# Last expert stage: the second part's row scatter waits for the shared network's last output

## The reference

```python
shared = new_gelu(xf @ Wfc_s + bfc_s) @ Wproj_s + bproj_s
logits = xf @ Wr
probs = jax.nn.softmax(logits, axis=-1)
topk_p, topk_i = jax.lax.top_k(probs, TOP_K)
topk_p = topk_p / jnp.sum(topk_p, axis=-1, keepdims=True)
...
for e in range(N_EXPERTS):
    h = new_gelu(xf @ Wfc[e] + bfc[e]) @ Wproj[e] + bproj[e]
    routed = routed + h * gate[:, e:e + 1]
return (shared + routed).reshape(Bb, Tt, C)
```

## Time and profile before

| | us |
|---|---|
| median of three runs | 6130.41 (6125.94 to 6135.96) |
| span of the profiled execution, first to last instruction | 6118.5 |
| this phase in it, first to last instruction | about 5434.7 to 6118.5 |
| shared network's last output (L1970) | 5706.85 |
| last tile's bias (L2144) | 6044.6 |

### The profile page before, as it was taken

One profiled execution on the slowest core, in us unless ns is written; L12 is line 12 of the kernel. 1 busy time (PEld: TensorE's weight loads), 2 busy tenths in 40 slices (PEclk: granted clock), 3 DMA queues, 4 the chain that ended last, 5 costly groups with the idle time before them and its releaser, 6 DMA issues. The chain is left out here.

```text
span 6118.5 us, 105868 instructions
## 1 busy us (share of the span) xinstructions
PE 5082.0 (83%) x38217; PEld 2622.6 (43%) x38217; DVE 3494.7 (57%) x5632; ACT 3177.6 (52%) x7160; POOL 2473.6 (40%) x2086
## 2 busy tenths in 40 slices
PE   6999789898977999997999999874237999974995
PEld 2444234344424666643566664442112222241784
DVE  5787422577845666643666654565338999730233
ACT  2666633366764666642566663342014888841552
POOL 3333000222216888831888871016562232116025
PEclk7999999799987999998999999886567999976997
DMA  3443111233410000020000000011112333211123
GB/s 102 111 119 111 41 45 50 64 103 107 115 32 20 8 7 6 5 82 19 8 6 6 7 3 4 2 42 27 36 35 68 90 90 97 59 46 49 52 78 91
DMA packets 329515, 312.95 MB, mean 51 GB/s; under 512 B 78758, under 2 KB 279106, under 8 KB 327106
## 3 DMA queue, kind: packets, MB, share of 16 engines
q1 hardware_dynamic: 312642, 285.77, 16.4%
q0 software_dynamic: 16384, 20.69, 1.3%
HBM read 172.15 MB, written 136.32 MB: 50 GB/s over the span
## 5 line engine op out<-in xcount | busy, mean ns | idle before, releaser
L806 ACT ACTIVATE a_prob<-a_PB 128x512 f32<-128x512 f32 x2304 | 1253.1, 597 | 453.0 <-PE a_PB L648 337.5
L696 PE MATMUL a_PO<-a_prob,a_V 128*32 128x256 f32 (+3 forms) x8192 | 713.3, 421 | 22.6 <-ACT a_cn L779 22.3
L960 DVE TENSOR_REDUCE a_blocks<-a_PA 128x8 f32<-128x1024 f32 x512 | 602.1, 1215 | 37.6 <-PE a_PA L648 35.1
L963 DVE TENSOR_REDUCE a_neg<-a_PA 128x2 f32<-128x1024 f32 x512 | 591.0, 1213 | 34.5 <-PE a_PA L661 34.5
L661 PE MATMUL a_PA<-a_KS,a_QS 48*128 48x512 bf16 (+3 forms) x3072 | 470.4, 345 | 109.7 <-DVE a_blocks L960 68.5
L2534 DVE TENSOR_REDUCE f1a_neg<-f1a_PA 128x2 f32<-128x384 f32 (+1 forms) x512 | 267.1, 522 | 489.1 <-PE f1a_PA L2336 488.6
L2464 POOL TENSOR_TENSOR f1a_prob<-f1a_prob,f1a_inv 128x384 f32<-128x384 f32 (+1 forms) x512 | 395.3, 775 | 283.4 <-DVE f1a_inv L2538 283.4
L678 PE MATMUL a_PB<-a_QS,a_KS 51*128 51x512 bf16 (+3 forms) x3072 | 447.7, 329 | 57.2 <-ACT a_prob L806 55.3
L2428 ACT ACTIVATE f1a_pt<-f1a_PT 128x512 f32<-128x512 f32 (+1 forms) x512 | 278.8, 544 | 348.5 <-PE f1a_PT L2345 344.8
L2421 ACT ACTIVATE f1a_prob<-f1a_PA,f1a_neg 128x192 f32<-128x192 f32 (+1 forms) x1024 | 406.2, 405 | 68.0 <-DVE f1a_neg L2534 67.9
L661 PEld LDWEIGHTS a_PA<-a_KS,a_QS 48*128 48x128 bf16 x3072 | 123.6, 94 | 632.8 <-DVE a_blocks L960 200.3
(11 more groups left out here) (422 smaller groups left out, 10380.5 us busy)
## 6 DMA issues: line engine op xcount, KB each, us to landing
a_spill<-a_qkp SPq DMA_DIRECT2D x96, 384.0 KB
a_QS<-a_spill SPq DMA_DIRECT2D x384, 96.0 KB, 2.5
a_KS<-a_spill SPq DMA_DIRECT2D x384, 96.0 KB, 2.5
a_spill<-a_qkp SPq DMA_DIRECT2D x96, 256.0 KB
a_raw<-a_cn SPq DMA_DIRECT2D x192, 72.0 KB
a_spill<-a_qkp SPq DMA_DIRECT2D x96, 128.0 KB
f_rows<-tokens_in SPq DMA_DIRECT2D x78, 128.0 KB
tokens_out<-f_rows SPq DMA_DIRECT2D x78, 128.0 KB
```

The lines of the kernel that those rows point to most:

```text
L696: mm = nc.tensor.matmul(PO[32 * j:32 * j + 32, first:last], V[:, par, t, 8 * e + pr], prob[:, k % st.ring, e, c + first - q0:c + last - q0 ...
L806: nc.scalar.activation(prob[:, k % st.ring, e], PB[:, ring_b.slot(0, ("b", s, e))], ACT.Exp, scale=scale).then_inc(pb_used, 1)
L960: nc.vector.tensor_reduce(to, of, AX, ALU.max).then_inc(pa_used, 1)
L963: nc.vector.tensor_reduce(neg[:, t, pr], PA[:, bank:bank + 2], AX, ALU.max, negate=True).then_inc(pa_used, 1)
```

## The change

POOL waits, between the 80 transfers of `scatter(0)` and the 48 of `scatter(1)`, until ACT has made all 16 outputs of the shared network.

```diff
             scatter(0)
+            pool.wait_ge(s_out, B)
             scatter(1)
             for h in range(2):
                 pool.wait_ge(scattered[h], 16 * 2 * tokens[h])
```

## The result

Median after: 6144.85 us (14 runs, 6131.76 to 6152.25), against 6133.50 for the kernel before, run beside it (14 runs, 6125.20 to 6136.47). The ratio is 1.0022 with a 95% interval of 1.0013 to 1.0030. I forecast 6126, an even trade; the kernel came out some 19 us above that, on the third rival's side. Of the 19, 3.1 us lie in the kernel before, which took 6133.50 beside it and 6130.41 when I worked out the forecast; the change itself cost 11.4 us between the medians.

A forecast was written before the change was run, and what follows sets the result against it. Unbroken indirect transfers were taken to slow the shared network to 0.29 of normal progress. Span 6118.5 - 45.5 gain + 41.2 cost = 6114.2, time 6126 us; 8-in-10 range 6107 to 6146.

The forecast's parts named there:

- Rival 1: Even trade: expert tiles lose between 33.2 and 57.8 us against the shared network's gain; time around 6126; chance 0.57.
- rival 3: Expert tiles nearly stand still beside a scatter stretched to 82.5 us: loss 69.4 us, time 6154.3; chance 0.15.
- The gain: Shared network: free rhythm after the first 80 scatters, last output at 5661.3 instead of 5706.85, 45.5 us gained.
- Loads and gathers not delayed: Expert tiles: the 48 scatters end about 5728, over 100 us before tile 47 needs them; cost nothing.
- The cost beside the tiles: 48 scatters beside the first expert tiles: 11.0 us for the first 16, 30.2 for the rest, 41.2 in all.
- p = 0.33: Share of normal progress the expert tiles keep beside the last 32 scatters, over 45.0 us; 30.2 us lost.
- 12-burst: 12 gathers beside tiles 53 to 56 in the old trace: at most 6.3 us lost.
- 16-burst: 16 gathers beside tiles 47 to 51 in the old trace: 11.0 us lost, taken as price of the first 16 scatters.
- The gathers' stretch "unchanged": Late expert tiles with gathers beside them, and the remaining gathers and stores: no change in time was priced.
- The signs: POOL idle some 60 us; outputs 6.87 us apart; beside scatters, tiles of 9 us and more, ten or so by 5732.
- Rival 2: Expert tiles suffer less, PE having work for a tile ahead: loss 25.2 us, time 6110.1; chance 0.23.
- Rival 4: The scatter isn't the cause of ACT's waits in the shared network: time 6130.4; chance 0.05.

The follow-up runs named there:

- doubled matmuls: Kernel before, every shared-network matmul in two halves of 256 columns, 32 instead of 16 a block: 6132.47 us in one run (before, beside it: 6119.12).
- doubled gelus: Kernel before, every shared-network gelu in two halves, 8 instead of 4 a block: 6135.52 us in one run (before, beside it: 6119.12).

## Why the prediction was off, step by step

**The gain: right.** 43.5 us for 45.5. The crawl ends with scatter 80, and the rhythm of 6.87 is back from output 7 on. What is missing are 2 us by which block 7's down product ended later: 120.2 us behind the first scatter, where the row on which I started the count had 118.2.

**Loads and gathers not delayed: right.** The 48 scatters end at 5719.94, 174 us ahead of the first gather.

**The cost beside the tiles: the failed step.** I wrote "in it the tiles progress at some rate p" and took p = 0.33 for the 32 transfers beyond the first 16. The term is 45.0 x (1 - p), and what was measured is 57.2 - 11.0 = 46.2, that is p = 0: the standstill that stood as my upper bound (56.0), and 1.2 us on top. What went wrong in it is, as far as the runs tell, the unit. I carried over progress as a share of the work, from a stage in which a block has 16 matmuls and takes 6.87 us to one in which a tile has 26 and takes 3.73. What carries over better is a number of matmuls per microsecond. Beside the shared network PE executed 68 + 54 = 122 matmuls in 164.7 us, 0.74 per us; beside the tiles 51 in 60 us, 0.85 per us. For a block 0.74 per us is 16 / 0.74 = 21.6 us, the crawl that was seen; for a tile it is 35 us, p = 0.11. With that the term would have been 45.0 x 0.89 = 40.1 and the cost 51.1, the time 6118.5 - 45.5 + 51.1 + 11.9 = 6136.0. The doubled matmuls bear the unit out for the shared network (0.59 and 0.62 matmuls per us in the stalled part, blocks of 23.6 and 50.1 us), and the doubled gelus, which change little, speak against the one that I used in rival 3. That it carries over to the tiles is a fit of counts and not shown: the two stretches above hold some free running, and without it the rates are 0.59 and 0.46; and in the kernel before most of PE's down products ran without a gap between waits for ACT, so its 0.59 is not a rate at which PE was held itself. With half the scatters beside the tiles the same count gave 20 us and 24.7 were lost. What is shown is that the tiles stood nearly still, and what holds them is open. A standstill is a little more than the count gives; 6 us of the 57.2 stay without a number.

I had the sign of this in hand. The 12-burst and the 16-burst together gave p = 0.1, in my own bounds, and I took the value between the other two because they were nearest in kind and in length. The two rows nearest in kind (tiles 49 and 50) lie in a burst of 16, and a burst of 12 cost 6.3 us at most; they show an average over the free part and the stalled part, not the rate in the stalled one.

**The gathers' stretch "unchanged": wrong by 9.5 us in the profiled execution.** Nothing in it was changed but its phase. In the other kernels in which gathers were left alone it took between 155.6 us (the small memset behind each scatter) and 167.1 (each scatter waits for the last one's landing), the kernel before at 157.8 and the one after at 167.3. A longer one is not tied to a longer loss in the tiles. I take it for a matter of where a burst falls in a tile, which is argued and not shown. A profile is one execution, so how much of the medians' difference lies there stays open too.

**The signs.** Outputs 6.9 us apart and POOL idle for 63 us came as written. "Ten or so" tiles by 5732 did not fit my own sum, which has about 21 us of undisturbed progress in the 62 us from the first bias at 5670, some six tiles. By that point, 240.4 us behind the first scatter, tile 0 alone had come (192.7); tile 1 came at 241.2 and tile 3 at 248.4, 18.6 us a tile and over the 15 that I had named as rival 3's sign.

**The rivals.** Rival 1 (even trade, loss under 57.8) holds for the loss, by 0.6 us. For the time it holds against the kernel before that ran beside it (11.4 us, under 12.3) and not against the 6130.41 of the forecast (14.4 us). Rival 2 falls: the work that PE had ahead didn't help, since PE itself stood. Rival 3 is right in kind, a near standstill. Its first reason, ACT's operations as the unit, has the doubled gelus against it; its second, single matmuls of PE with gaps before them, is what the rows after show. Its size was not reached: it took a scatter of 82.5 us and a loss of 69.4, and the scatter took 65.4 us and the loss was 57.2. Rival 4 falls by every experiment: the memset behind each scatter alone took 114 us off the shared network. With it goes the rule of the Trainium skill (SBUF — State Buffer, "Who interferes with whom") that PE and ACT never wait on anyone, if it is read as a promise about time: it speaks of the ports, and this trace shows ACT idle for 24.0 us in one piece beside POOL's transfers.

**The range** held the median, 1 us inside its upper end.

## What to carry to other kernels

A disturbance that is moved is paid for in the unit in which it takes, and that unit has to be found first: count what got through per microsecond (matmuls, operations, transfers) in the disturbed stretch, set it against what the new neighbour needs, and not against the time that it takes undisturbed, and keep a standstill inside the range. And before a streak of indirect transfers is moved, try to break it up: two in flight instead of all at once cost one semaphore more for each part and gave 1.3% here, and 1.7% with the gathers, where none of the places tried for the unbroken streak gave anything.

## What the runs showed of the hardware

- Indirect scatters that POOL issues 1.28 us apart, one after the other, hold the other engines nearly still: in the stalled part PE executes 0.59 matmuls per us of 2.3 (shared network) and 0.46 of 7.0 (tiles). Beside the tiles (kernel after) PE stood 13.5 us into the streak, behind 11 transfers; beside the shared network (kernel before) ACT stood behind 18 and PE behind 22. It ends about 3 us behind the last transfer. In the run with halved matmuls it ended inside the streak, with a step of 4.0 us between two transfers.
- A little room between them is enough. At 1.9 and 2.3 us apart, and at an average near 1.57 with never more than two in flight, there was no stall of scatters, neither beside the shared network nor beside the tiles; groups of eight at 1.28 us, with 3.0 us from a group's last to the next one's first, left the shared network alone and cost the tiles 15 us.
- The bytes are not the reason: 42 GB/s with two in flight and no stall, 47 to 51 GB/s with it, and 72 GB/s of loads and stores in the quiet tiles. PE's waits inside one product, 2.1 to 2.8 us from matmul to matmul, are not for a semaphore of the program. Nor do the packets point to slow loading of code: the traces list packets of the kind "instruction", of 16 KB, and the one in the kernel before's stall took 1.39 us and the one beside the tiles after 1.36 us, where those of the quiet tiles after took 0.88 to 1.43 us; a wait ahead of such a packet would not be seen. Which part of the chip the engines share with such transfers no run here shows. No run had plain transfers in such a streak, and every execution on record was traced, so that a part of the tracing itself in it isn't excluded.
- The granted clock falls to 0.55 of 2.4 GHz while PE stands (0.68 beside the shared network), so a part of what little gets through runs at the lower of the two levels, 1.2 GHz. With two in flight it is 1.00 in the same stretch. That is a consequence here: a single matmul's 0.37 us is small against the gaps.
